# Attention maxima turned on VectorE instead of TensorE, in a fused attention and mixture-of-experts block

## What is computed

```
xn = layernorm(x)
q, k, v = xn @ Wq.T, xn @ Wk.T, xn @ Wv.T          # 16 heads of 16
q, k = rope(q, k)
scores = einsum(q, k) / 4, causal
attn = softmax(scores) @ v ;  a = attn @ Wo.T
moe = sum over the 4 best experts of weight * down(silu(gate(xn)) * up(xn))
shared = silu(xn @ sgate.T) * (xn @ sup.T) @ sdown.T
out = x + a + moe + shared
```

## Time and profile before

| | |
|---|---|
| median of three runs | 2096.0 us |
| profiled execution | 2089.78 us, span 2088.0 us |
| TensorE busy in the span | 1800.1 us, 86% |
| VectorE busy | 1377.0 us, 66% |
| ScalarE busy | 758.2 us, 36% |
| GpSimd busy | 998.2 us, 48% |
| mean granted TensorE clock | 0.927 of full speed |
| TensorE in 150 to 240 us (the loop) | 84.34 of 90 us |
| VectorE in the same stretch | 64.84 of 90 us |

### The profile page before, as it was taken

One profiled execution on the slowest core, in us unless ns is written; L12 is line 12 of the kernel. 1 busy time (PEld: TensorE's weight loads), 2 busy tenths in 40 slices (PEclk: granted clock), 3 DMA queues, 4 the chain that ended last, 5 costly groups with the idle time before them and its releaser, 6 DMA issues. The chain is left out here.

```text
span 2088.0 us, 41196 instructions
## 1 busy us (share of the span) xinstructions
PE 1800.1 (86%) x10415; PEld 1092.9 (52%) x10416; DVE 1377.0 (66%) x3411; ACT 758.2 (36%) x1667; POOL 998.2 (48%) x993
## 2 busy tenths in 40 slices
PE   5898999999999999999999999995999999999300
PEld 2354554545545455454554545543888888888300
DVE  6667668667686675866767667651566666666487
ACT  2334333342343423334234342331444444444200
POOL 5455445553454534545345453473555555555200
PEclk8999999999999999999999999976999999999755
DMA  6251541624506246052460624565555555556499
GB/s 136 78 123 37 108 93 39 127 50 87 111 26 121 54 84 111 27 124 45 90 111 29 121 49 86 104 185 197 150 167 170 168 178 167 172 170 181 136 352 326
DMA packets 217741, 255.29 MB, mean 122 GB/s; under 512 B 74421, under 2 KB 166334, under 8 KB 217536
## 3 DMA queue, kind: packets, MB, share of 16 engines
q1 hardware_dynamic: 160000, 161.90, 33.8%
q0 software_dynamic: 35840, 71.63, 10.7%
q10 hardware_dynamic: 21824, 20.98, 3.1%
HBM read 112.54 MB, written 94.64 MB: 99 GB/s over the span
## 5 line engine op out<-in xcount | busy, mean ns | idle before, releaser
L715 DVE TENSOR_REDUCE neg<-ps_u 128x2 f32<-128x768 f32 (+3 forms) x384 | 391.5, 1044 | 149.7 <-PE ps_u L935 145.4
L494 POOL DMA_INDIRECT table<-entry,slot x256 | 254.4, 994 | 360.6 <-ACT xs L578 260.0
L1204 POOL DMA_INDIRECT y_dram<-yb,ent x288 | 283.4, 984 | 223.5 <-issue 169.7
L496 POOL DMA_INDIRECT values<-xs,slot x256 | 248.6, 971 | 83.3 <-issue 83.3
L915 PE MATMUL ps_g<-we_gu 128*128 128x512 f32 x512 | 243.6, 609 | 0.0
L600 ACT ACTIVATE probs<-ps_u 128x1024 f32<-128x1024 f32 x160 | 159.3, 1021 | 160.0 <-PE ps_u L973 159.6
L600 ACT ACTIVATE we_d<-ps_u 128x1024 f32<-128x1024 f32 x160 | 161.1, 1022 | 152.5 <-PE ps_u L973 152.3
L962 PE MATMUL ps_u<-q_st,k_st 50*128 50x512 f32 (+3 forms) x1024 | 171.6, 394 | 50.7 <-DMA q_st<-neg_t 14.7
L931 PE MATMUL ps_u<-k_st,q_st 48*128 48x128 f32 (+3 forms) x1024 | 185.6, 400 | 31.1 <-DVE neg L715 20.7
L481 POOL TENSOR_TENSOR we_d<-we_d 128x512 f32<-128x512 f32 x64 | 81.3, 1271 | 211.4 <-DVE we_d L685 208.6
L931 PEld LDWEIGHTS ps_u<-k_st,q_st 48*128 48x128 f32 x1024 | 88.2, 189 | 168.2 <-issue 74.2
(11 more groups left out here) (157 smaller groups left out, 3012.7 us busy)
## 6 DMA issues: line engine op xcount, KB each, us to landing
xg<-values SPq DMA_DIRECT2D x288, 128.0 KB
ys<-y_dram SPq DMA_DIRECT2D x64, 512.0 KB, 5.5
q_st<-we_gu SPq DMA_DIRECT2D x192, 128.0 KB, 7.7
k_st<-we_gu SPq DMA_DIRECT2D x192, 128.0 KB, 9.5
we_gu<-x SPq DMA_DIRECT2D x16, 512.0 KB, 6.0
xres<-x SPq DMA_DIRECT2D x16, 512.0 KB, 5.4
sum_dram<-osum SPq DMA_DIRECT2D x16, 512.0 KB, 4.7
we_gu<-wgu_e ACTq DMA_DIRECT2D x16, 512.0 KB, 5.0
```

The lines of the kernel that those rows point to most:

```text
L494: pool.indirect_dma_start(table[:, :], bass.IndirectOffsetOnAxis(ap=slot[:, k:k + 1], axis=0), entry[:, k, :], None).then_inc(scattered, 16)
L496: pool.indirect_dma_start(values[:, :], bass.IndirectOffsetOnAxis(ap=slot[:, k:k + 1], axis=0), xs[:, k // TOPK, :], None).then_inc(scatte ...
L715: nc.vector.tensor_reduce(neg[:, g % 2, i, :, k0:k0 + nk], ps[:, :, 0:nk * n].rearrange("p a (k n) -> p a k n", n=n), AX.X, ALU.max, negat ...
L1204: pool.indirect_dma_start(y_dram[:, :], bass.IndirectOffsetOnAxis(ap=ent[k][:, 0:1], axis=0), yb[k][:, :], None, bounds_check=TOKENS * TOP ...
```

## The change

The four matmuls of `negT` and ScalarE's copy are gone, and with them `ident_r`. `negT` stays in the list for SyncE alone, which has its two DMAs at the same place. `negsplit` on VectorE goes on, after L727, with four transposes of 32 x 32 float32 blocks, one per 32 partitions of `neg_p`, each written to partitions 0 to 31 of `neg_t` at another 32 columns. Ahead of the first stand a wait for `neg_parts`, VectorE's own split, and one for `neg_rows`, the DMAs of the group two before. The columns of `neg` and `neg_p` are ordered anew so that a DMA now reads 16 partitions with runs of 128 floats (512 bytes) where it read 4 partitions with runs of 512 floats. `negT` takes no bank of `ps_g` any more, so that the others go round differently.

```diff
-        neg = sb("neg", [P, 2, NT, 2, 2])
-        neg_p = sb("neg_p", [P, 2, NT, 2, NPART, 2], F32R)
-        neg_t = sb("neg_t", [NPART * GH, 2, SEQ])
+        neg = sb("neg", [P, 2, 2, 2, NT])
+        neg_p = sb("neg_p", [P, 2, 2, NPART, 2, NT], F32R)
+        neg_t = sb("neg_t", [32, 2, P])
...
                     sp.dma_start(q_st[HALF * a + KROWS:HALF * a + MROWS, 2 * g:2 * g + 2, :].bitcast(F32),
-                                 neg_t[4 * a:4 * a + 4, g % 2, :]).then_inc(neg_rows[g % 2], 16)
+                                 neg_t[16 * a:16 * (a + 1), g % 2, :]).then_inc(neg_rows[g % 2], 16)
...
-            def negT(b, step, env):                                     # ScalarE
-                g, bank = step[1], env[0][step, 0][0]
-                act.wait_ge(pe["negT"], NG * b + g + 1)
...
-                nc.scalar.activation(neg_t[:, g % 2, :].bitcast(F32R), ps_g[bank][0:NPART * GH, 0:SEQ],
-                                     ACT.Copy).then_inc(S["neg_t"], 1)
...
             def negsplit(b, step, env):                                 # VectorE
...
                 nc.vector.tensor_tensor(np_[:, :, 1, :], n_, np_[:, :, 0, :].bitcast(F32), ALU.subtract
                                         ).then_inc(neg_parts, 1)
+                dve.wait_ge(neg_parts, NG * b + g + 1)
+                if g >= 2:
+                    dve.wait_ge(neg_rows[g % 2], NEG_ROWS * (2 * b + g // 2))
+                else:
+                    dve.wait_ge(neg_rows[g % 2], NEG_ROWS * 2 * b)
+                for lo in range(0, P, 32):
+                    ins = nc.vector.transpose(neg_t[:, g % 2, lo:lo + 32], flat[lo:lo + 32, :])
+                ins.then_inc(S["neg_t"], 1)
...
-            def negT(b, step, env):                                     # TensorE
...
-                for t in range(NT):
-                    ins = nc.tensor.matmul(ps[0:NPART * GH, t * P:(t + 1) * P],
-                                           neg_p[:, g % 2, t, :, :, :].rearrange("p a r k -> p (a r k)"), ident_r[:],
-                                           start=(t == 0), stop=(t == NT - 1), skip_group_check=True)
-                ins.then_inc(pe["negT"], 1)
```

More of the change, by code:

```diff
@@ L56 @@
 TABLE = E * REGION + P
-N_CONSTS, N_EARLY, N_IDENT = 24, 22, 4
+N_CONSTS, N_EARLY, N_IDENT = 23, 21, 3
 SKIP = 1 << 24
@@ L126 @@
      ("rank",), ("rankA",), ("rankB",)]
-BANKS_OF = {"gate": ("gated",), "up": ("hidden",), "negT": ("neg_t",), "xT": ("xn_t",), "qk": ("rope",),
+BANKS_OF = {"gate": ("gated",), "up": ("hidden",), "xT": ("xn_t",), "qk": ("rope",),
             "vr": ("logits",), "tables": ("cos_t", "sin_t"), "rank": ("ranked",)}
@@ L309, in phase_a @@
             sem("neg_parts"), sem("tanh_done"), sem("av_out"), sem("exps"), sem("chosen_ready")
-        pe = {n: sem("pe_" + n) for n in ("xT", "tables", "qk", "vr", "gate", "up", "s1", "negT", "s2", "av", "sum", "rank")}
+        pe = {n: sem("pe_" + n) for n in ("xT", "tables", "qk", "vr", "gate", "up", "s1", "s2", "av", "sum", "rank")}
         dve_front, dve_chain, ex_ready, rope1, rope2 = \
@@ L316, in phase_a @@
         SCATTERS = 2 * 16 * NT * TOPK
+        NEG_ROWS = 16 * 2
         def done(name, b, k):
@@ L632, in _ @@
             run(act, {"loaded": loaded, "xT": xT, "tables": tables, "vr": qkv, "gate": gate, "copy": copy, "part0": part0,
-                      "placeV": place_v, "negT": negT, "s2": s2,
+                      "placeV": place_v, "s2": s2,
                       "exps": exponentials, "load_gu": load_gu, "load_d": load_d})
@@ L714, in s1 @@
                 dve.wait_ge(pe["s1"], NG * NU1 * b + NU1 * g + u + 1)
-                nc.vector.tensor_reduce(neg[:, g % 2, i, :, k0:k0 + nk],
+                nc.vector.tensor_reduce(neg[:, g % 2, :, k0:k0 + nk, i],
                                         ps[:, :, 0:nk * n].rearrange("p a (k n) -> p a k n", n=n), AX.X, ALU.max,
@@ L721, in negsplit @@
                 dve.wait_ge(S["row_max"], done("row_max", b, NU1 * g + NU1 - 1))
-                dve.wait_ge(pe["negT"], NG * b + max(0, g - 1))
+                dve.wait_ge(S["neg_t"], NG * b + g)
                 dve.wait_ge(neg_parts, NG * b + g)
-                n_ = neg[:, g % 2, :, :, :].rearrange("p t a k -> p (t a) k")
-                np_ = neg_p[:, g % 2, :, :, :, :].rearrange("p t a r k -> p (t a) r k")
+                n_ = neg[:, g % 2, :, :, :].rearrange("p a k t -> p a (k t)")
+                np_ = neg_p[:, g % 2, :, :, :, :].rearrange("p a r k t -> p a r (k t)")
+                flat = neg_p[:, g % 2, :, :, :, :].rearrange("p a r k t -> p (a r k t)").bitcast(F32)
                 back.link(b, nc.vector.tensor_copy(np_[:, :, 0, :], n_))
@@ L956, in s2 @@
                 if u == 0:
-                    pe_.wait_ge(neg_rows[g % 2], 32 * (2 * b + g // 2 + 1))
+                    pe_.wait_ge(neg_rows[g % 2], NEG_ROWS * (2 * b + g // 2 + 1))
                 for lo, kt, k in S2_PIECES[u]:
@@ L1037, in _ @@
             run(pe_, {"loaded": loaded, "xT": xT, "tables": tables, "qk": qk, "vr": vr,
-                      "gate": hidden_part("gate", 0), "up": hidden_part("up", 1), "s1": s1, "negT": negT, "s2": s2, "av": av_,
+                      "gate": hidden_part("gate", 0), "up": hidden_part("up", 1), "s1": s1, "s2": s2, "av": av_,
                       "down": down, "oproj": oproj, "rank": rank})
```

9 lines of the change are left out of this document (removed).

## The result

The changed kernel took 2143.77 us (median of 4 runs, 2143.37 to 2146.57) and the kernel before 2097.03 us (4 runs, 2092.29 to 2103.26): a ratio of 1.0212, with an interval of 1.0184 to 1.024. It is 47 us slower, and 14 us above the upper end of the predicted range.

What follows compares the result with a forecast made beforehand. The loop waits for TensorE, busy 86%, taking turns with VectorE within a batch. +10 us over the engines and +5 us for the clock, beside the median 2096.0, gave 2110 us in round numbers; range 2084 to 2130.

Steps and rivals of the forecast that it cites:

- The sum over the engines: Whole loop: added delays less savings over four groups, +0.68 us a batch, +10 us over 15 batches.
- the term for the clock: Whole loop: added TensorE stalls bring more time at the lower clock, in proportion to the waits, estimated +5 us.
- The transposes: VectorE's `negsplit`: four new 32 x 32 transposes do not overlap, take 0.97 us and delay what follows by 1.05 us.
- The row with the change of partitions: Profile row of L683 after L682 on VectorE: operations on other partitions did not overlap, so transposes start 0.25 us apart.
- d: Delay the four transposes add to VectorE's later work in each group: 1.05 us, or 0.55 if they overlap.
- the gain of some 14 us: Whole change, by the skill's cost table at 0.09 us a transpose; the prediction said the profile rows disagree.
- Group 0: Third `xT` waits for the late `hid` 3, and the 0.33 us saved on TensorE is lost: +0.75 us a batch.
- Group 1: `s2` 1,0 waits for VectorE's later maxima: +0.42 us a batch.
- Group 3: Transposes and two DMAs replace the old path to `s2` 3,0: -0.16 us a batch.
- The sum without the clock: Per batch: 0.75 + 0.42 - 0.33 - 0.16 = +0.68 us, +10 us over 15 batches.
- groups 2 and 3: Later maxima at group 2 are covered, -0.33 us a batch; the start of `s2` 3,0 at group 3 gains, -0.16.
- a rival: New wait at `xT` draws low clock in every batch, 1 to 2 us each: 2122 to 2140 us; chance 12%.

Runs made afterwards that it cites:

- change, one transpose: The changed kernel with one 128 x 32 VectorE transpose in place of four, three of four blocks of maxima not reaching their place: 2079.83 us.
- change, other order: The changed kernel with `s1` 1,3 moved ahead of `xT` 1 and `vr` 0 ahead of `s1` 1,4: 2124.4 us.
- change, fill at `xT`: The changed kernel with one dummy matmul of 512 columns, its result never read, added ahead of `xT` 1: 2126.93 us.
- change, three fills: The changed kernel with dummy matmuls of 512 columns added ahead of `xT` 1, `av` 2 and `s2` 3,0: 2125.67 us.
- change, moves and fills: The changed kernel with `s1` 1,3, `vr` 0 and `s2` 1,0 moved in TensorE's list and dummy matmuls ahead of six of its waits: 2063.74 us.
- change, fills only: The changed kernel in its own order, with dummy matmuls ahead of `xT` 1 and six other TensorE waits: 2080.18 us.

## Why the prediction was wrong

The sum over the engines, +10 us, came out at an estimated 11; the term for the clock, +5 us, at some 44. The steps in their order:

- **The transposes: right.** The row with the change of partitions was the right one to go by. Four take 0.84 us, a fifth of a microsecond each, and they do not overlap; d was predicted as 1.05 us and is 1.02. The Trainium skill's rule ("VectorE: DVE Perf Modes", section "Two Vector instructions with no wait between them") agrees. The estimate from its table of costs, 0.09 us for one, does not: the profile shows 0.20, and the gain of some 14 us that this would have given did not come. The Trainium skill itself says beside that table (same page, section "The TRN2 errata") that its VectorE row comes out too low for a single operation.
- **Group 0: right in kind, short in size.** The batch of the earlier trace rows begins, on ScalarE's timeline of the kernel before, at 916.56, and the next one at 1002.35:

```profile
916.56 1.05 ACT L559 ACTIVATE v_pad<-we_gu 128x1024 f32<-128x1024 f32 x1
...
1002.35 1.05 ACT L559 ACTIVATE v_pad<-we_gu 128x1024 f32<-128x1024 f32 x1
```

  The stall is at the `xT` that wait for VectorE's readers, but it is at two of them and not at the third alone, since `gth` 3 too is late for its bank. After, `s1` 1,3 starts 22.49 us into the batch (252.80 less 230.31); before, 21.24 us (937.80 less 916.56). That is 1.25 us later and not 0.75; 0.2 of it is half of the 0.4 us that the low stretch has lasted by then, which leaves 1.05.
- **Group 1: right.** `s2` 1,0 waits 0.42 us for the maximum, as predicted, and the delay grows there by 0.34 us (below). That `s1` 2,1 would wait longer for its exponential, 0.70 in place of 0.23 us, was not.
- **Group 3: right in the sum, wrong in the rows.** I had the two waits become one. They stayed two, with an exponential in the place of the split; the DMAs took 2.80 us from the end of the transposes (296.84 to 299.64), against 2.84.
- **The sum without the clock: right.** The two batches just compared are 89.37 and 85.79 us long; apart from the stretch of 6.8 us each has one of 3.4. The delay can be followed through them, as the start after less the start before, each from its batch's marker. The second `vr` is one more point; before, it was

```profile
942.86 1.13 PE L905 MATMUL ps_g<-we_gu 128*128 128x288 f32 x4
```

  The delay is 1.25 us at `s1` 1,3; 3.83 at the second `vr` (30.13 against 26.30), where the low stretch is over; 4.17 at `s2` 1,0 (39.26 against 35.09); 3.60 at `s2` 3,0 (69.33 against 65.73); and 3.58 at the end. So the stretch cost 3.83 - 1.25 + 0.2, about 2.8 us, and what is left is 1.05 at group 0, 0.34 at group 1 and -0.57 at groups 2 and 3 (predicted 0.75, 0.42 and -0.49): +0.82 us a batch, where 0.68 was predicted. Over 14 batches that is an estimated 11 us, from one pair of batches, where the sum had 10.
- **The clock: the step that failed.** The term was +5 us, in proportion to the added waits. Of the 55.9 us some 44 remain for it by the working above, with 119.5 us more of low time. The text had the mechanism as a rival ("If the new wait at `xT` draws a low stretch in every batch, it costs 1 to 2 us a batch: 2122 to 2140") and gave it 12%. It happened, but the stretch cost 2.8 us, and the second stretch of each batch, longer than before in five of them, added to it: about 3.2 us a batch. To reckon in proportion to the wait was the fault: the waits were to grow by half, and the low time grew by a factor of 2.4. The base was too small as well. I took the 1.0 us by which the mean batch is longer than the fastest for all that the clock cost; but the fastest batches hold a stretch of 3.4 us too, and the low time before is 85.3 us in 14 batches, 6.1 us in each.

Batch and low time go together over the kernels that were run. In the last column half of the low time, the most that it can cost if half the clock does half the work, is taken off the mean batch:

| kernel | batch us | low time in 14, us | batch less half of low / 14 |
|---|---|---|---|
| before | 86.31 | 85.3 | 83.26 |
| after | 90.30 | 204.8 | 82.99 |
| before, four transposes more | 89.50 | 160.4 | 83.77 |
| change, one transpose | 85.93 | 85.3 | 82.88 |
| change, other order | 88.62 | 174.1 | 82.40 |
| change, fill at `xT` | 88.77 | 150.2 | 83.41 |
| change, three fills | 88.75 | 139.9 | 83.75 |
| change, moves and fills | 84.83 | 20.5 | 84.10 |
| change, fills only | 85.58 | 0 | 85.58 |

The last column lies between 82.3 and 84.5 us for all but the last row, and for the eight kernels that are not in the table too. It is no constant, and half is too much. Within a kernel, a straight line through its 14 batches rises by 0.24 to 0.44 us for each us of low time, in each of the 16 kernels that have any; the 44 us for 119.5 are 0.37. A long stretch that spans the waits of group 3 costs least: between the two kinds of batch after the change the low time differs by 10.3 us and the length by 2.3.

Which waits come ahead of the second stretch can be seen in the batch shown above:

```profile
286.64 0.44 PE L928 MATMUL ps_u<-k_st,q_st 48*128 48x384 f32 x2 [0.40 <-DVE neg L703]
...
288.35 0.50 PE L949 MATMUL ps_u<-q_st,k_st 50*128 50x512 f32 x2 [0.28 <-DVE neg L703]
...
289.48 0.51 PE L949 MATMUL ps_u<-q_st,k_st 50*128 50x384 f32 x4 [0.41 <-DVE neg L703]
```

These are `s1` 3,3, `s2` 2,1 and `s2` 2,2, and the clock is low from 289.9 us, ahead of both long waits of group 3 (296.1 and 299.6). The kernel before has the same three waits. The kernel with three fills leaves them open and has its stretch of 10.2 us there; the one with fills only fills these three, and `s2` 0,2, and has no low time. So that stretch hangs on the short waits of groups 0 and 2, which these runs do not tell apart, and not on the long ones of group 3.

What stays open is which wait makes the clock fall in a given batch. Nearly all stretches begin 20 to 23 us into the batch or 54 to 71 us in, and they come and go from batch to batch. The first came with the other order without the stall at `xT`, and with one transpose at group 0 behind a wait of 0.29 us there; the second stays away in the first four batches of the kernel before, though it has the same waits. That TensorE's idle time brings them follows from the fills, which add only busy time; how much idle time at which place does it was not settled.

## What to carry to other kernels

Where TensorE is busy above 90% of a loop, price an edit by whether its new waits, of half a microsecond or so, bring a stretch of low clock into every pass, and price that stretch at a quarter to a half of its own length, beside the sum over the engines. Check it by adding up the time at low clock per pass, and when it is there, move work into the waits or fill them with dummy matmuls before judging the edit: the same change read +2.1% bare, and level with the kernel before when both had the same moves and fills and nearly all of their clock. Small VectorE operations that each start on other partitions come one after the other, and four short ones cost a microsecond.

## What the runs showed of the hardware that was not expected

- More work was faster: one dummy matmul of 1.02 us in a batch gave 17 us, and seven gave 64 us (2143.8 to 2080.2), with no time at low clock in 14 batches.
- A low stretch outlasts its wait many times. After 2.40 us of which TensorE was idle 0.93 came 6.8 us at 0.50, in which TensorE was busy throughout, and then by 1.00.
- The pattern locks to the batch: mostly 89.4 and 91.7 us in turn after the change, and 88.7 to 88.8 us in 12 of the 14 batches of the kernel with three fills. This fits that a delay of a microsecond is not worth a microsecond here, and that either half of the transposes taken away gave back more than half of the loss; it was not tested by itself.
